# The centre tap of a depthwise convolution is computed on another engine: eight tiles per group move from ScalarE to VectorE

## What is computed

```
x = x + xattn(layernorm(x), ctx)               # projections with low-rank terms, two softmaxes
x = x + ffn(layernorm(x))
# ffn:
h = bit_linear(x, w1)                          # activations quantised per token, ternary weights; 256 -> 1024
h = depthwise_conv1d(h, conv_w, conv_b)        # three taps along the tokens, per channel, plus a bias
h = silu(h)
y = bit_linear(h, w2)                          # 1024 -> 256
```

## Time and profile before

| what | value |
|---|---|
| median of 3 runs | 1510.79 us (1509.88 to 1510.84) |
| the profiled execution | 1510.81 us |
| its span, first to last instruction | 1508.8 us |
| PE / DVE / ACT / POOL busy | 1406.3 / 1200.7 / 1168.3 / 667.0 us |
| TensorE clock granted, mean | 0.982 of full |
| centre taps on ACT (L776) | 128 of them, 113.7 us busy |

### The profile page before, as it was taken

The page is one execution under the profiler, slowest core; times in us unless marked ns, Lnnn a source line. Parts: engine busy times, 40 slices in busy tenths (PEclk is TensorE's granted clock), DMA queues, the critical chain, the costliest instruction groups (busy, mean ns, idle before and its releaser), DMA issues.

```text
span 1508.8 us, 33043 instructions
## 1 busy us (share of the span) xinstructions
PE 1406.3 (93%) x10604; PEld 1162.3 (77%) x10650; DVE 1200.7 (80%) x3074; ACT 1168.3 (77%) x3894; POOL 667.0 (44%) x1058
## 2 busy tenths in 40 slices
PE   7899999999999999999999999999999999999762
PEld 4688878888788888878787888888788788878541
DVE  4364698788879878897888888788888878788888
ACT  3487897978878797887879788887978788797832
POOL 2354444545344444534445454444445444453520
PEclk9999999999999999999999999999999999999985
DMA  9210100011010100001010000001000100100000
GB/s 277 60 31 16 32 16 28 20 29 30 15 44 15 44 1 29 30 28 31 15 44 1 28 30 29 30 15 44 14 17 29 29 30 15 44 1 14 17 15 14
DMA packets 41144, 47.13 MB, mean 31 GB/s; under 512 B 3024, under 2 KB 35216, under 8 KB 41104
## 3 DMA queue, kind: packets, MB, share of 16 engines
q1 hardware_dynamic: 41104, 46.62, 10.3%
HBM read 36.13 MB, written 10.49 MB: 31 GB/s over the span
## 4 chain that ended last, share of the span: by engine, by line
PE 48%; DVE 29%; ACT 13%; issue 8%; DMA 1%; DVEq 0%; POOL 0%; SPq 0%; POOLq 0%; ACTq 0%
PE PS L501 10%; PE PS L444 7%; PE PS L463 6%; PE PS L514 6%; ACT SM L754 5%; PE PS L479 5%; PE PS L488 5%; PE PS L453 4%; DVE HP L1002 2%; PE PS L592 2%; DVE GBS L1088 2%; DVE HP L1008 2%; PE PS L613 2%; DVE MX L913 2%; DVE HP L1024 1%
## 5 line engine op out<-in xcount | busy, mean ns | idle before, releaser
L1240 POOL TENSOR_TENSOR SM<-SM,RC 128x496 f32<-128x496 f32 (+1 forms) x512 | 324.2, 654 | 721.2 <-DVE RC L907 721.2
L754 ACT ACTIVATE SM<-PS,MX 128x124 f32<-128x124 f32 x1024 | 360.0, 370 | 157.8 <-DVE SM L915 155.8
L501 PE MATMUL PS<-KT,QM 128*128 128x128 f32 x2048 | 276.8, 278 | 20.7 <-ACT SM L754 20.6
L501 PEld LDWEIGHTS PS<-KT,QM 128*128 128x128 f32 x2048 | 249.4, 192 | 32.6 <-ACT SM L754 31.9
L754 ACT ACTIVATION_READ_ACCUMULATOR SM<-PS,MX 128x1 f32 x1024 | 216.3, 211 | 0.0
L1271 POOL TENSOR_TENSOR OTl<-OF,OTh 128x256 fp32r<-128x256 f32 x256 | 203.1, 793 | 10.4 <-ACT OF L748 10.4
L488 PE MATMUL PS<-IDF,SM 128*128 128x128 f32 x1024 | 167.9, 287 | 16.0 <-POOL SM L1240 15.9
L913 DVE TENSOR_REDUCE MX<-PS 128x4 f32<-128x496 f32 x256 | 170.0, 664 | 0.0
L479 PEld LDWEIGHTS PS<-PT,V 128*64 128x64 f32 x2048 | 106.6, 136 | 82.2 <-issue 75.6
L479 PE MATMUL PS<-PT,V 128*64 128x128 f32 x2048 | 168.5, 285 | 0.0
L746 ACT ACTIVATE OTh<-PS 128x256 fp32r<-128x256 f32 x256 | 100.3, 392 | 84.9 <-PE PS L479 83.9
(11 more groups left out here) (166 smaller groups left out, 3514.9 us busy)
## 6 DMA issues: line engine op xcount, KB each, us to landing
XIN<-in_x SPq DMA_DIRECT2D x16, 512.0 KB, 3.5
XRES<-in_x SPq DMA_DIRECT2D x16, 512.0 KB, 4.2
out_y<-HP SPq DMA_DIRECT2D x15, 512.0 KB, 3.2
CRAW<-in_ctxT SPq DMA_DIRECT2D x16, 256.0 KB, 2.6
RRAW<-in_ctxT SPq DMA_DIRECT2D x32, 128.0 KB, 2.8
QM<-in_Wq SPq DMA_DIRECT2D x1, 1024.0 KB, 9.3
GBS<-in_Wo SPq DMA_DIRECT2D x1, 1024.0 KB, 13.9
k_ipa_columns<-HP SPq DMA_DIRECT2D x1, 1024.0 KB, 6.5
```

The costliest lines, as they stand in the source:

```text
L501: m = mm(psS[:, h, :], QM[:, 2 * q + h // 2, h % 2, TOK * b:TOK * b + TOK], KT[:, 2 * q + h // 2, b, :], start=True, stop=True)
L754: m = act.activation(SM[s % 2][:, h, 0:ORG], psS[:, h, 0:ORG], ACT.Exp, bias=MX[s % 2][:, h:h + 1], accum_out=SU[s % 2][:, h:h + 1])
L1240: m = pool.tensor_tensor(part, part, RC[c % 2][:, 4 * i:4 * i + 4].unsqueeze(2).broadcast_to(shape), ALU.mult)
```

## The change

The centre taps of all eight tiles are made by DVE in every group but the last, with one `tensor_scalar` each: in GB, times CW (a per-partition scalar), plus CB (another one), out to HT. Its completion counts a new semaphore, `t1v_done`, for which `conv_before` waits. T1_DVE would leave the first tiles on ACT; it is 0.

```diff
+T1_DVE = 0
@@ ScalarE, finish
                 j = tile_at(n - M_F1 - M_LAG[0])
-                if 0 <= j < CT:
+                if 0 <= j < (CT if is_last(g) else T1_DVE):
                     act.wait_ge(g_done, g.count(CT, j + 1))
@@ VectorE
             def conv_before(g, j):
-                dve.wait_ge(t1_done, g.count(CT, j + 1))
+                if is_last(g):
+                    dve.wait_ge(t1_done, T1_DVE * g.off + j + 1)
+                elif j < T1_DVE:
+                    dve.wait_ge(t1_done, g.count(T1_DVE, j + 1))
+                else:
+                    dve.wait_ge(t1v_done, g.count(CT - T1_DVE, j + 1 - T1_DVE))
+            def centre(g, j):
+                dve.wait_ge(g_done, g.count(CT, j + 1))
+                if j < NB:
+                    need(dve, out_done, g.count(16, 0))
+                dve.tensor_scalar(HT[j].rearrange("p (b t) -> p b t", b=NB), GB[j % 4], CW[:, j, 1:2], CB[:, j:j + 1],
+                                  ALU.mult, ALU.add).then_inc(t1v_done, 1)
@@ VectorE, finish, behind the multiplication of a tile (L1064)
+                j = tile_at(n - M_F1 - M_LAG[0])
+                if T1_DVE <= j < CT:
+                    centre(g, j)
                 j = tile_at(n - M_F1 - M_LAG[2])
                 if 0 <= j < CT:
                     conv_next(g, j)
```

More of the change, by code:

```diff
@@ L272, in program @@
         q1t_full, q1t_done, bc_full, bc_done = (sem(n) for n in ("q1t_full", "q1t_done", "bc_full", "bc_done"))
-        f1_full, g_done, t1_done, t2_done, t3_done, th_done, h_done = (
-            sem(n) for n in ("f1_full", "g_done", "t1_done", "t2_done", "t3_done", "th_done", "h_done"))
+        f1_full, g_done, t1_done, t1v_done, t2_done, t3_done, th_done, h_done = (
+            sem(n) for n in ("f1_full", "g_done", "t1_done", "t1v_done", "t2_done", "t3_done", "th_done", "h_done"))
         hm_done, ht_full = sem("hm_done"), sem("ht_full")
```

## The result

| | median us | range | runs |
|---|---|---|---|
| before | 1510.82 | 1509.88 to 1511.42 | 4 |
| after | 1548.17 | 1547.06 to 1549.24 | 4 |

The ratio is 1.0247, 95% interval 1.0231 to 1.0263: 37.4 us slower, where 16 were forecast. The direction was right, the size was less than half of what was measured; the time lies near where the first rival (GpSimd is in the way, 1545) put it.

What follows compares the result with a forecast made beforehand. In the tile stretch PE, DVE and ACT hand the end to each other. Per group 3.96 us added on DVE, less 1.92 absorbed and 0.98 of ACT's relief, leaves 1.06; times 15 groups, 16 us on 1510.8 gives 1527 us (range 1510 to 1556).

Steps and rivals of the forecast that it cites:

- the first rival: In the tile stretch GpSimd holds up one tap in four by 0.585 us: 18 us, 1545 us; chance 0.16.
- The price of a tap: On DVE in the tile stretch, one tap costs 0.454 us as a step, about 0.54 us as a row.
- the rival with the slow rate: On DVE each tap costs 0.73 instead of 0.454 us: 33 us more, 1560 us; chance 0.12.
- The three readers directly behind: On DVE, three of eight taps have their reader directly behind, costing 0.11 us more each.
- What is absorbed: DVE's waits inside the tile stretch, with the overlap that comes back, take up 1.92 us of added work a group.
- ACT's relief: At the exponentials ending the tile stretch, ACT's shorter queue gives back 0.98 us a group.
- the deciding place: DVE's small step before ACT's exponentials at 740.78: DVE 2.04 us later, exponentials and PE's scores 1.06 us later.
- What DVE gets back at the tanh: At the last gate, DVE's 1.4 us wait takes in part of its lateness: about 1.06 us late, not 2.04.
- That delays earlier in the stretch are swallowed: PE's delays from new taps earlier in the stretch add nothing, as PE is still behind ACT's exponentials at 742.
- The stalls: GpSimd's hold-ups of DVE rows in the tile stretch were taken as unchanged, adding nothing to the sum.

Runs made afterwards that it cites:

- e7: Changed kernel with T1_DVE = 6, only the taps of tiles 6 and 7 on DVE: 1501.65 us.
- e6: Changed kernel with T1_DVE = 7, only the tap of tile 7 on DVE: 1500.58 us.
- e5: Changed kernel with its eight DVE taps replaced by reductions of 360 elements, the centre tap itself left out: 1532.96 us.
- e8: Changed kernel with T1_DVE = 4, the taps of tiles 4 to 7 on DVE: 1515.17 us.
- e2: Changed kernel with GpSimd's four residual additions moved from halves 16 to 22 to halves 28 to 31, behind the tile stretch: 1535.51 us.
- e9: Kernel before, plus six unused reductions of 360 elements a group on DVE ahead of tile 0's multiplication: 1511.74 us.
- e11: Changed kernel with only the taps of tiles 6 and 7 on DVE and GpSimd's residual additions moved behind the tile stretch: 1505.02 us.

## Why the prediction was wrong, step by step

*The price of a tap: right.* 0.454 us as a step and 0.54 as a row; the row is 544 ns, and where nothing holds it up the next instruction starts 0.45 us behind it (729.23 to 729.68). The fast rate holds with an output step of two, so the rival with the slow rate fell. The Trainium skill's 1.71 ns a column (Vector Engine (DVE) Microarchitecture Reference, section 5.2) is for an output that hops 4 KiB every element; carried over to a step of two, as the forecast's estimate did, it would have made the tap 0.34 us longer, and no such time shows.

*The three readers directly behind: right.* The next instruction starts about 0.04 us behind the tap's end (727.38 + 0.54 to 727.96 at tile 0), 0.03 was used.

*What is absorbed: right.* 1.92 us of waits; e7 would be later at the place by 1.02 - 0.80 = 0.22 and is by 0.21, e6 earlier by 0.35 and is by 0.34.

*ACT's relief and the deciding place: right in size.* 0.98 forecast, 3.38 - 2.45 = 0.93 in the changed kernel, and 0.88 to 0.92 in e5, e7 and e8. What releases PE there was told incompletely: the exponentials are in time to within 0.1 us, but PE waited for POOL's scaling first (1.01 us). Both hang on DVE.

*What DVE gets back at the tanh: right in sum, wrong in its parts.* The forecast let nearly 1 us of DVE's lateness fall into its wait of 1.4 us for the tanh. DVE does get 0.93 us back between the place and the last gate, but the wait shrinks only from 1.40 to 1.28 us. The greater part is that the stalls behind the place went from 0.79 to 0.15 us.

*That delays earlier in the stretch are swallowed: held up.* PE's longer wait for DVE at the W1 product, 14.3 us in the run, does not show in the period beyond the lateness of the place.

*The stalls: the step that failed.* The sum took them as unchanged ("a stall hits whichever instruction is there, and the POOL operations do not become more"). Over the run they rose by a fifth: 48.9 instead of 40.8 us. But the sum needed those ahead of the place, and they rose from 1.87 to 3.20 us a group. The lateness was put at 2.04 and is 3.38; the difference of 1.34 is the 1.33 of the stalls. Before, about 0.8 us of them lay behind the place (2.7 in all, 1.87 ahead), where DVE waited for the tanh anyway. The reason given did not hold, although the POOL operations did not become more: the taps are themselves held up (1.10 us, in three of eight), and with them in the queue POOL's low part and its addition each catch a row of DVE where one gate had met both, which holds up `conv_before` by 0.98 us where nothing had; against this, `conv_next` is no longer held up (0.76 us before). With the risen stalls, the sum is 1.06 + 1.33 = 2.4 us a group, 36 us, 1547. The term stood among the rivals as one tap in four held up at 0.585 us (18 us, 1545) with a chance of 0.16, though the fast form was known to meet POOL (L855, up to 815 ns). That the rival's time came so near is in part luck: it counted the taps alone, two a group, and the 1.33 us are what is left of several changes, of which the taps are one. e5 and e2 take away one part each, 1.15 and 1.06 us ahead of the place; they overlap, since the sum of both is more than 1.33.

## What to carry over

An engine's free time is worth something only where it lies: 2.7 us of reductions were free at one place (e9) and eight taps, or eight such reductions (e5), dear at another. Moving just the one instruction that the other engine waits for (T1_DVE = 7) gains 10.3 us (1510.9 to 1500.6); a second one adds nothing, four cost 4 us and eight 37; three were not measured. When instructions with two SBUF inputs or in a fast form are added where GpSimd works too, count the stalls ahead of the place that decides, and price them as part of the sum.

## What the hardware did that I had not expected

The reduction of 360 elements (one input, 509 to 532 ns in 120 of 120) is never held up by GpSimd, while the fast one-input form of 544 ns goes up to 1030, as the gate with two inputs goes from 686 to 1230. The multiplication of a tile, which has two inputs as well, but one of them in PSUM, takes 673 to 692 ns in all 120 rows, and in 45 of them beside an operation of POOL. This agrees with what the GPSIMD Engine Reference of the Trainium skill says in its key points, contention with DVE instructions in a two-port mode or with two SBUF inputs; a row that is held up takes between 0.14 and 0.56 us more in the group shown. And an operation of GpSimd that is moved out of a stretch can do more harm where it lands: 0.40 us on the last gate in e11.
